# Attention with routed experts on one core: weight and value sums of a batch gathered, reciprocals spread in row tiles, the engines' orders rewritten

## The reference

```python
xn = layernorm(x)                                   # per token
Q = xn @ Wq.T + bq; K = ctx @ Wk.T + bk; V = ctx @ Wv.T + bv     # 16 heads of 32
attn = softmax(Q K^T / sqrt(32)); out = attn @ V
x = x + tanh(g_xattn) * ((mean over 8 experts (out @ We.T + be)) @ Wo.T + bo)
logits = layernorm(x) @ w_gate; best = argmax(logits) per token
# each expert takes its first 100 tokens, in order over all batches
x = x + tanh(g_ffn) * gate * (layernorm(x) @ w_expert + b_expert)   # taken tokens only
```

## Time and profile before

| | |
|---|---|
| median of 3 runs | 405.21 us (405.14 to 405.38) |
| the profiled execution | 405.64 us, its span 403.9 us |
| busy: TensorE, VectorE, ScalarE, GpSimd | 396.3, 333.3, 225.3, 167.4 us |
| share of TensorE and VectorE in the span | 98%, 83% |
| granted TensorE clock | 1.00 |

### The profile page before, as it was taken

One profiled execution on the slowest core, in us unless ns is written; L12 is line 12 of the kernel. 1 busy time (PEld: TensorE's weight loads), 2 busy tenths in 40 slices (PEclk: granted clock), 3 DMA queues, 4 the chain that ended last, 5 costly groups with the idle time before them and its releaser, 6 DMA issues.

```text
span 403.9 us, 8706 instructions
## 1 busy us (share of the span) xinstructions
PE 396.3 (98%) x3102; PEld 182.2 (45%) x3102; DVE 333.3 (83%) x662; ACT 225.3 (56%) x320; POOL 167.4 (41%) x157
## 2 busy tenths in 40 slices
PE   7999999999999999999999999999999999899996
PEld 4556454443444444444444434444444444354444
DVE  6548456986898989998998998899897589779996
ACT  4436323568566754947485486748556474775110
POOL 2028999215080247309033530713271064460371
PEclk9999999999999999999999999999999999999999
DMA  8999991466059408823960692295169016241585
GB/s 278 334 389 394 344 390 41 91 124 165 2 111 199 174 1 170 217 98 85 175 223 1 142 238 104 60 183 189 54 133 242 5 33 175 84 132 28 99 172 180
DMA packets 65901, 63.19 MB, mean 156 GB/s; under 512 B 42277, under 2 KB 45617, under 8 KB 65859
## 3 DMA queue, kind: packets, MB, share of 16 engines
q1 hardware_dynamic: 60747, 56.19, 50.9%
q0 software_dynamic: 1632, 3.49, 3.1%
q10 hardware_dynamic: 3480, 2.96, 2.2%
HBM read 29.59 MB, written 12.98 MB: 105 GB/s over the span
## 4 chain that ended last, share of the span: by engine, by line
PE 71%; DVE 2%; issue 1%; ACT 1%; POOL 1%; DVEq 0%; ACTq 0%; POOLq 0%
PE ps L840 71%; ACT probs L1234 1%; PE ps L1161 0%; DVE xb L1567 0%; POOL known L1929 0%; POOL rstd L1929 0%; DVE bn_raw L1573 0%; ACT xn_hi L1234 0%; DVE xn L1500 0%; DVE base_cnt L1653 0%; DVE place_hot L1723 0%; POOL veps L1927 0%; ACT part_x L1234 0%; DVE xb L1865 0%; DVE wqT_lo L1678 0%
## 5 line engine op out<-in xcount | busy, mean ns | idle before, releaser
L1234 ACT ACTIVATE probs<-ps 120x1024 f32<-120x1024 f32 x64 | 62.0, 1024 | 19.4 <-PE ps L840 19.4
L1602 DVE TENSOR_REDUCE neg_max<-ps 128x16 bf16<-128x1920 f32 x32 | 68.7, 2148 | 3.7 <-PE ps L840 3.7
L1989 POOL TENSOR_TENSOR attn_lo<-attn,attn_hi 128x512 f16<-128x512 f32 x28 | 31.8, 1158 | 91.0 <-ACT attn_hi L1234 91.0
L840 PE MATMUL ps<-xnT_hi,wqT_hi 128*128 128x512 f16 x128 | 48.6, 380 | 0.0
L840 PE MATMUL ps<-mixT_hi,attn_hi 128*128 128x512 f16 x128 | 48.5, 379 | 0.0
L840 PE MATMUL ps<-mixT_lo,attn_hi 128*128 128x512 f16 x128 | 48.5, 379 | 0.0
L840 PE MATMUL ps<-xnT_lo,wqT_hi 128*128 128x512 f16 x128 | 48.5, 379 | 0.0
L1997 POOL TENSOR_TENSOR xb<-xb,mix_bias 128x512 f32<-128x512 f32 x32 | 39.6, 1271 | 15.4 <-DVE cb_col L1544 15.4
L1234 ACT ACTIVATE q_hi<-ps,bias_cols 128x512 f16<-128x512 f32 x32 | 22.1, 692 | 31.4 <-PE ps L840 31.4
L840 PE MATMUL ps<-q_stack,k_stack 97*128 97x512 f16 x128 | 33.9, 381 | 1.2 <-ACT probs L1234 1.0
L840 PE MATMUL ps<-probs,den_sel 120*32 120x256 f32 x512 | 34.1, 384 | 0.0
(11 more groups left out here) (279 smaller groups left out, 792.7 us busy)
## 6 DMA issues: line engine op xcount, KB each, us to landing
xb<-in_x_dram SPq DMA_DIRECT2D x8, 1024.0 KB, 6.1
q_stack<-q_hi SPq DMA_DIRECT2D x48, 128.0 KB, 2.4
out_dram<-xb SPq DMA_DIRECT2D x6, 1024.0 KB, 7.4
raw<-in_L_xattn_We_dram SPq DMA_DIRECT2D x5, 1024.0 KB, 10.3
q_stack<-q_lo SPq DMA_DIRECT2D x32, 128.0 KB, 2.4
xb<-in_L_xattn_We_dram SPq DMA_DIRECT2D x3, 1024.0 KB, 10.3
k_stack<-k_scratch SPq DMA_DIRECT2D x8, 360.0 KB, 4.6
k_scratch<-k_hi ACTq DMA_DIRECT2D x16, 120.0 KB, 7.9
```

The source lines that it names most:

```text
L840: return e.matmul(out_, a, b, start=start, stop=stop, **kw)
L1234: return e.activation(out_, in_, func, **kw)
L1602: e.tensor_reduce(maxed[:, :, :, g], quad[:, :, 0:NT * SK].rearrange("p j (t s) -> p t j s", t=NT), AX.X, ALU.max, negate=True).then_inc(s ...
L1989: e.tensor_tensor(attn_lo[:, g, :], attn[:, g, :], attn_hi[:, g, :], ALU.subtract).then_inc(s_alo, 1)
```

## The change

`probs` gets four buffers for all batches but the last, so that `all_weight_sums` and the four `value_sums` of a batch follow each other behind the scores; the values go to the four banks of `quad`. `rows` lies in the buffers of `probs`, and is no longer cleared. The weight sums are taken by token tiles of 128 (`SQ`) where it was halves of 256, so the reciprocal has 128 columns and not 256. `spread_all` spreads them by 16 products in row tiles, between value sums 2 and 3. Query tiles 0 to 2 stand among the scores, tile 3 around the sums. The low part of x is made by GpSimd (`x_low`, with the waits of `x_lo`). `route_x` writes `den_b`; places and table share `num_b` with the logits. Scores 3 wait for maxima 0 of the next batch, and value sums for its maxima 1. `scores(0, 0)` goes behind the last prepared unit, ahead of `gate_mix`. The lists of all engines are rewritten; the last batch keeps its own (with `head_sel` by token tiles). Cut to its core:

```diff
-        den_sel = sb("den_sel", [SK, 2 * NK * DK + 24], F32)
-        head_sel = sb("head_sel", [P, 2, NK, P], F16)
+        den_sel = sb("den_sel", [SK, 2 * DK + NK], F32)
+        head_sel = sb("head_sel", [P, NT, NK, P], F16)
+        head_of = sb("head_of", [P, NT, HJ], F32)
+        spread_sel = sb("spread_sel", [P, NT, P], F16)
...
-        probs = sb("probs", [SK, 2, HJ, S], F32)
+        probs = sb("probs", [SK, NK, HJ, S], F32)
+        rows = probs[0:CAP, 2:NK, :, :].rearrange("p g j s -> p (g j) s")
         attn = sb("attn", [P, NK, S], F32)
-        rows = sb("rows", [CAP, NE, D], F32)
         attn_hi = sb("attn_hi", [P, NK, S], F16)
         attn_lo = sb("attn_lo", [P, NK, S], F16)
-        rden = sb("rden", [P, SH], F32)
-        rden_hi = sb("rden_hi", [P, SH], F16)
-        rden_both = sb("rden_both", [P, SH], F16)
+        rden = sb("rden", [P, SQ], F32)
+        rden_hi = sb("rden_hi", [P, SQ], F16)
+        rden_both = sb("rden_both", [P, SQ], F16)
...
-        def places_bank(b):
-            return den_b if b == B - 1 else num_b if b == B - 2 else g0_b
-
-        table_b = g1_b
+        def places_at(b):
+            first = NT * 2 * NE + NW * NE if b < B - 2 else 0
+            return (den_b if b == B - 1 else num_b)[:, first:first + NT * NE]
+
+        def table_at(b, cols):
+            first = NT * 2 * NE if b < B - 3 else 0
+            return (num_b if b < B - 3 else g1_b)[0:CAP, first + cols.start:first + cols.stop]
 
         def last_bank(i):
             return num_b if i == NT else quad[:, i, :]
 
         def route_bank(b):
-            return g0_b if b else num_b
+            return den_b if b else num_b
 
         def value_bank(b, g):
-            return quad[:, 3, :] if (b, g) == (B - 1, 3) else num_b
+            return quad[:, g, :] if b < B - 1 else quad[:, 3, :] if g == 3 else num_b
+
+        def spread_bank(b, g):
+            return (quad[:, 0, :], quad[:, 1, :], den_b, num_b)[g] if b < B - 1 else (den_b, num_b)[g % 2]
+
+        MAX_AHEAD = 2
+
+        def probs_slot(b, g):
+            return g if b < B - 1 else g % 2
...
+                    if g == 3 and b < B - 1:
+                        e.wait_ge(s_mx, 4 * (b + 1) + 1)
...
+            def all_weight_sums(b, _):
+                e.wait_ge(s_ex, 4 * b + 4)
+                e.wait_ge(s_pxe, b + 2)
+                steps = [(t, j) for t in range(NT) for j in range(HJ)]
+                for t, j in steps:
+                    first = SEL_AT - (2 * t * NK + j)
+                    for g in range(NK):
+                        ins = mm(den_b[g * DK:(g + 1) * DK, 0:SQ], den_sel[:, first:first + DK],
+                                 probs[:, g, j, t * SQ:(t + 1) * SQ],
+                                 start=((t, j) == steps[0]), stop=((t, j) == steps[-1]))
+                ins.then_inc(s_den, 1)
 
             def value_sums(b, g):
                 if (b, g) == (B - 1, 3):
                     e.wait_ge(s_ex, 4 * B)
                 elif (b, g) == (B - 1, 0):
                     e.wait_ge(s_plr, B - 1)
+                elif b < B - 1:
+                    e.wait_ge(s_mx, 4 * (b + 1) + MAX_AHEAD)
...
+                if b and g == 0:
+                    e.wait_ge(s_ex, 4 * b - 1)
+                elif b and g < MAX_AHEAD:
                     e.wait_ge(s_ex, 4 * b)
+                elif b:
+                    e.wait_ge(s_at, 4 * (b - 1) + 2)
+                    e.wait_ge(s_num, 4 * b)
...
+            def spread_all(b, _):
+                e.wait_ge(s_rhi, b + 1)
+                e.wait_ge(s_rlo, b + 1)
+                e.wait_ge(s_num, 4 * b + 2)
+                if b == 0:
+                    prologue_over(e)
+                e.wait_ge(s_lraw, b)
+                e.wait_ge(s_plr, b)
+                e.wait_ge(s_tab, max(0, b - 1))
+                for t in range(NT):
+                    for g in range(NK):
+                        row = slice(g * DK, (g + 1) * DK)
+                        ins = mm(spread_bank(b, g)[:, t * SQ:(t + 1) * SQ], spread_sel[row, t, :], rden_both[row, :])
+                        if t == NT - 1:
+                            ins.then_inc(s_bc, 1)
...
-                (q_tile, 1, 0), (q_begin, 1, 1), (max_scores, 1, 0), (q_end, 1, 1), (route_x, 1, 0), (q_tile, 1, 2),
-                (max_scores, 1, 1),
-                (q_tile, 1, 3), (max_scores, 1, 2), late_unit(0), (max_scores, 1, 3), late_unit(1), (max_turn, 1, 0),
-                late_unit(2), late_unit(3), (scores, 1, 0), late_unit(4), late_unit(5),
+                (q_tile, 1, 0), (q_begin, 1, 1), (max_scores, 1, 0), (route_x, 1, 0), (q_end, 1, 1),
+                (q_tile, 1, 2), (max_scores, 1, 1), (q_tile, 1, 3), (max_scores, 1, 2), late_unit(0), late_unit(1),
+                late_unit(2), (max_scores, 1, 3), late_unit(3), (max_turn, 1, 0), late_unit(4), late_unit(5),
+                (scores, 1, 0),
             ])
             run(range(0, B - 2), [
-
-                (logits, -1, 0), (table_rows, -2, 0), (scores, 0, 1), (values, 0, 0), (scores, 0, 2),
-                (values, 0, 1), (route_x, 1, 0), (scores, 0, 3), (q_begin, 1, 0), (gate_mix, 0, 0),
-                (q_end, 1, 0), (places, -1, 0), (values, 0, 2), (values, 0, 3), (max_scores, 1, 0),
-
-                (q_tile, 1, 1), (q_begin, 1, 2), (spread_rden, 0, 0), (spread_rden, 0, 1), (q_end, 1, 2),
-                (max_scores, 1, 1), (spread_rden, 0, 2), (spread_rden, 0, 3), (q_tile, 1, 3),
-
-                (mix_high, 0, 0), (max_scores, 1, 2), (mix_low, 0, 0), (mix_high, 0, 1),
-                (max_scores, 1, 3), (route_attn, 0, 0), (mix_low, 0, 1), (mix_begin, 0, 2), (max_turn, 1, 0),
-                (mix_middle, 0, 2), (mix_low, 0, 2), (mix_high, 0, 3), (scores, 1, 0), (mix_low, 0, 3),
+                (gate_mix, 0, 0), (scores, 0, 1), (logits, -1, 0), (q_tile, 1, 0), (scores, 0, 2), (q_tile, 1, 1),
+                (max_scores, 1, 0), (q_tile, 1, 2), (table_rows, -2, 0), (scores, 0, 3), (route_x, 1, 0),
+                (places, -1, 0), (q_begin, 1, 3), (max_scores, 1, 1), (all_weight_sums, 0, 0), (value_sums, 0, 0),
+                (value_sums, 0, 1), (value_sums, 0, 2), (spread_all, 0, 0), (value_sums, 0, 3), (q_end, 1, 3),
+                (max_scores, 1, 2), (mix_high, 0, 0), (max_scores, 1, 3), (mix_low, 0, 0), (mix_high, 0, 1),
+                (max_turn, 1, 0), (mix_low, 0, 1), (route_attn, 0, 0), (mix_high, 0, 2), (mix_high, 0, 3),
+                (scores, 1, 0), (mix_low, 0, 2), (mix_low, 0, 3),
             ])
...
-                e.wait_ge(s_val, max(0, 4 * b + g - 1))
+                e.wait_ge(s_val, max(0, 4 * (b - 1) + g + 1 if b < B - 1 or g < 2 else 4 * b + g - 1))
                 to_logit = 1.0 / (QK_SCALE * QK_SCALE * float(DK) ** 0.5)
-                act(probs[:, g % 2, 0:2, :], quad[0:SK, 0:2, :], ACT.Exp, scale=to_logit).then_inc(s_ex2, 1)
+                act(probs[:, probs_slot(b, g), 0:2, :], quad[0:SK, 0:2, :], ACT.Exp, scale=to_logit).then_inc(s_ex2, 1)
                 e.wait_ge(s_sc, 4 * b + g + 1)
-                act(probs[:, g % 2, 2:4, :], quad[0:SK, 2:4, :], ACT.Exp, scale=to_logit).then_inc(s_ex, 1)
+                act(probs[:, probs_slot(b, g), 2:4, :], quad[0:SK, 2:4, :], ACT.Exp, scale=to_logit).then_inc(s_ex, 1)
...
-                (exp, 0, 1), (value_out, 0, 0), (exp, 0, 2), (x_hi, 2, 0), (value_out, 0, 1), (x_hi, 2, 1),
-                (route_x_out, 1, 0), (x_hi, 2, 2), (exp, 0, 3), (gate_mix_high, 0, 0), (q_high, 1, 0), (x_hi, 2, 3),
-                (value_out, 0, 2), (value_out, 0, 3), (gate_exp, -1, 0),
-
-                (rden_high, 0, 0), (q_high, 1, 1), (attn_high, 0, 0), (q_high, 1, 2), (attn_high, 0, 1),
-                (attn_high, 0, 2), (attn_high, 0, 3), (q_high, 1, 3),
-
-                (stack_q, 1, 0), (stack_q, 1, 1), (shift_row, 1, 0), (part_high, 0, 0), (exp, 1, 0),
+                (exp, 0, 1), (gate_mix_high, 0, 0), (q_high, 1, 0), (exp, 0, 2), (q_high, 1, 1), (x_hi, 2, 0),
+                (exp, 0, 3), (route_x_out, 1, 0), (q_high, 1, 2), (x_hi, 2, 1), (value_out, 0, 0),
+                (rden_high, 0, 0), (gate_exp, -1, 0), (value_out, 0, 1), (x_hi, 2, 2), (x_hi, 2, 3),
+                (value_out, 0, 2), (attn_high, 0, 0), (value_out, 0, 3), (attn_high, 0, 1), (attn_high, 0, 2),
+                (q_high, 1, 3), (attn_high, 0, 3), (stack_q, 1, 0), (shift_row, 1, 0), (part_high, 0, 0),
+                (stack_q, 1, 1), (exp, 1, 0),
...
+            heads = ident[:, :].rearrange("p (b t c j) -> p t j b c", b=NK, t=NT, c=2)
+            for t in range(NT):
+                e.tensor_reduce(head_of[:, t, :], heads[:, t, :, :, :], AX.XY, ALU.add).then_inc(s_setv, 1)
+            e.wait_ge(s_setv, SETV - 3)
+            e.tensor_copy(spread_sel[:, :, :].rearrange("p t (j d) -> p t j d", d=DK),
+                          head_of[:, :, :].unsqueeze(3).to_broadcast([P, NT, HJ, DK])).then_inc(s_setv, 1)
...
+                e.wait_ge(s_num, 4 * b + g + 1)
```

(60 more changed lines are left out.)

178 lines of the change are left out of this document (86 added, 92 removed).

## The result

The changed kernel takes 428.13 us (427.31 to 429.47, 4 runs) against 405.29 us of the kernel before on the same chip: a ratio of 1.057, 95% interval 1.055 to 1.059. The forecast was 407.1 us. Its own range ended at 409.5 and its highest rival at 414. It had the side right and the size wrong by 21 us.

The account below looks back on a forecast made before the run. TensorE bounds the kernel: -0.6 us of work and +1.1 of waits make a batch 36.5 us; batches 1 to 5 +2.5, with the ends +1.9 in all, so 407.5 profiled, 407.1 median; range 406 to 409.5.

Parts of the forecast that it names:

- TensorE's part (a, b, c): Per batch: spread gains 0.66 us, weight sums in quarters 0, changes of tile shape cost 0.12; together -0.6 us.
- (b): Weight sums as 64 products of 128 columns instead of 32 of 256 still flow: 0 us, bounds -0.1 and +0.3.
- Rival 3: Half-length weight sums don't flow, +1 us a batch, 413 us; chance 0.09 together with late transfers.
- Relief elsewhere: VectorE loses some 3.3 us a batch, idle GpSimd gains 4.5 us of subtractions; worth nothing in itself.
- Points 1 and 2: TensorE's waits in a batch: scores 3 for maxima(1,0), 0.33 us; weight sums behind exp 3 and route_x_out, 0.15 us.
- Point 4: ScalarE's queue behind the spread: TensorE waits 0.5 us for attn_high 3; maxima(1,2) adds 0.1, GpSimd's fourth attn_low 0.15.
- Point 5: scores(1,0) wait 0 to 0.3 us, taken as 0.1, behind q_hi and q_lo issues and shift; x_hi's transpose causes none.
- Rival 2: Transfers of x's low half or q_stack rows land after their use: 409.5 to 414 us; chance 0.09 together with sums.
- Ahead of batch 0: gate_mix waits for ScalarE's and VectorE's copies of the gate product, +0.3 us; set-up +0.1.
- Batch 6: -0.6 us, one stay fewer -0.2, extra 0.7 gone, less 0.8 for maxima product 2 waiting on value_out 3: -0.7.
- the 0.7 us of the logits: Batch 6's extra 0.7 us of before, taken as a wait for late logits that the change removes.
- Last stretch: Last batch: third exponential hangs on VectorE's last moments, expert_low now stands behind them: -0.3 us, bounds 0 and -1.

Follow-up runs that it names:

- e10: The kernel before with only the weight sums in quarters: 64 products of 128 columns a batch instead of 32 of 256; 405.63 us, ratio 0.999 to 1.001.
- e2: The changed kernel with GpSimd's bias additions moved from the head of its list to behind rstd1; 418.67 us.
- e8: e2 plus add_table behind maxima(1,0), q_lo issues on ScalarE's queue, stack_q 1 ahead of part_high, attn_high 3 ahead of q_high 3; 418.84 us.
- e1: The changed kernel with gate_value and enter_rows moved back behind part_low on VectorE in batches 0 to 5; 418.90 us.
- e3: The kernel before with gate_value and enter_rows moved ahead of maxima(1,2) on VectorE, beside GpSimd's bias additions; 424.54 us.
- e4: e3 with GpSimd's bias additions also moved ahead of rstd2, early in the batch; 435.80 us.

## Why the prediction was wrong

**TensorE's part (a, b, c): right.** Spread and weight sums came within 0.05 us, and e10 confirms (b) by itself. Rival 3, sums that don't flow, falls as a rate. What I didn't list is that a stretch of short instructions can break off (some 2 us in the last batch); that it outruns its supply is my reading, not shown.

**The term that failed** is one sentence under "Relief elsewhere": GpSimd's four more subtractions on an engine idle for 23 us, "worth nothing in itself". They moved the bias additions later, the change moved enter_rows earlier, and the two met. I costed GpSimd's list by its own free time and VectorE's small operations at their durations of before, with no row asked which instructions of the two ran at the same time. In the kernel before the additions end at 227.8 and enter_rows begins at 233.0; the layout would have shown the meeting, had I written both down. Measured: 2.5 us of wait in each of four batches, and 1.7 of clock in three of them, 15 of the 22 us. Undoing it gave 9.2 to 9.5, since waits of 0.8 to 2.1 us a batch then came out, one of them, in e2, from the additions' next meeting.

**Points 1 and 2: right** to 0.05 us in batch 3 (0.30 and 0.15), up to the held writes. **Point 4: right in its sum by luck.** It had 0.5 us for attn_high 3 and 0.1 for maxima(1,2); measured are 0.15 and 0.39. What binds there is the path product, reduction, product of 2.7 us, which I never added up against the eight products beside it, and e8, built on my reading, gained nothing. **Point 5: mis-sized.** I took 0.1 us for scores(1,0). The six q_hi issues took 4.1 to 5.2 us in batches 3 to 5 instead of the 3.7 of the earlier trace rows (batch 3 of the changed kernel below), and the wait was 0.4 to 1.2 us; the gap and the slow clock hid most of it in the changed kernel, e1 and e2 show it.
```profile
231.56 5.16 SPq L743 DMA_DIRECT2D q_stack<-q_hi  x6
```
Rival 2 had the mechanism and no place for it in the forecast.

**Ends.** Ahead of batch 0: +0.95 instead of +0.4. Batch 6: +1.0 instead of -0.7. The 0.9 us behind value sums 3 came as said (0.8), but the 0.7 us of the logits, which I had as gone, stayed: it was never a wait. Eight 32-bit products make them in that batch, 0.81 us before (338.07 to 338.88) and 0.91 after, where the 16-bit ones of the other batches take 0.2. A wait of 0.3 us ahead of `places` was new, and some 0.6 us I can't place. Last stretch: +2.8 instead of -0.3, of which some 2 are the breaks.

The sum, then: +1.9 forecast, +22.1 measured; by the trace 15 from the held writes and their clock, 2.8 from the end, the rest in mis-sized waits and the two ends of the batches; by experiment 9.2 to 9.5 come back when the meeting is undone. The range missed because all its cases were sums over single engines and queues; no case had two engines in each other's way.

## What to carry over

Before moving work to an idle engine, write down what runs beside it at its new place, and beside all that it pushes: here an addition of 8 elements cost a microsecond because GpSimd was in a 512-column subtraction. Small VectorE operations from SBUF belong beside GpSimd's pauses, VectorE's PSUM reads beside its long instructions. Where VectorE reduces between two products, the path through it is added up against the products beside it. And a stretch of very short TensorE instructions can break off where its columns don't say so.

## What the runs showed of the hardware

- Held beside a long GpSimd instruction, to its end: VectorE's TENSOR_SCALAR, TENSOR_TENSOR and SCALAR_TENSOR_TENSOR from SBUF (small ones 0.17 to 0.22 us alone, up to 1.3 beside an addition, 2.5 beside a clearing that reads nothing; a normalisation of 128x512 1.36 and 1.55 instead of 0.54). Not held: what reads PSUM (0.68 to 0.74), reductions (0.18), statistics (0.68), the reciprocal (0.18). GpSimd's four additions took 4.93 to 4.96 us in the changed kernel and the one before, with or without held writes beside them, and 5.1 to 5.3 in most batches of e2, e3 and e4.
- One wait of 2.5 us in an otherwise full stretch was followed by 3.41 us at the 1.2 GHz level in three cases of four.
- Queue 8 of the DMA records has loads of 16 KB, 0.9 to 2.4 us each, one for some 256 of TensorE's instructions. In stretches of such short instructions as the weight sums and the products of 8 columns TensorE broke off for up to 0.5 us in some runs, and in one it went on in groups of 8 to 18 instructions every 0.7 us; that a missing load is the cause is not shown.
- Six equal issues of SyncE took 3.7 us in most batches and up to 4.9 (old order) and 5.2 (new order) in others; what decides it stayed open.
